# Eight-core recurrence and ternary layer: transposing DMAs issued by ScalarE, and the fourth pair's statistics taken earlier

## The reference

```
xn  = (x - mean(x)) / sqrt(var(x) + 1e-5)            # per row
a   = tanh(xn @ Wa.T + ba);  b = tanh(xn @ Wb.T + bb)  # [4096, 64]
h_t = a_t * h_(t-1) + b_t                            # a scan over the 4096 rows
y1  = xn + h @ Wout.T + bout
s   = mean(|weight|)                                 # weight [2048, 2048]
w_t = clip(round(weight / (s + 1e-10)), -1, 1) * s
y   = x + y1 + xn @ w_t.T + bias
```

## Time and profile before

| What | us |
|---|---|
| Runs: median (lowest to highest of 3) | 548.99 (546.73 to 550.02) |
| The profiled execution's own time | 545.46 |
| Its span, slowest core (core 3) | 543.9 |
| Spans of the other cores | 535.8 (core 0) to 543.6 (core 7) |
| TensorE busy, core 3 | 467.0 (86% of the span) |
| VectorE, ScalarE, GpSimd busy | 341.8, 215.8, 150.3 |
| SyncE's DMA queue, share of 16 engines' span | 61.3% |
| TensorE waiting in front of gate products, core 3 | 12.4 in 5 waits |

### The profile page before, as it was taken

One profiled execution on the slowest core, in us unless ns is written; L12 is line 12 of the kernel. 1 busy time (PEld: TensorE's weight loads), 2 busy tenths in 40 slices (PEclk: granted clock), 3 DMA queues, 4 the chain that ended last, 5 costly groups with the idle time before them and its releaser, 6 DMA issues.

```text
span 543.9 us, 8281 instructions; the slowest of 8 cores (535.8 to 543.9 us)
## 1 busy us (share of the span) xinstructions
PE 467.0 (86%) x2323; PEld 223.9 (41%) x2323; DVE 341.8 (63%) x516; ACT 215.8 (40%) x183; POOL 150.3 (28%) x536
## 2 busy tenths in 40 slices
PE   0020489999939999999999999999999999999997
PEld 0010134545424444444444545454545444545443
DVE  2633497969737574857576767666666757573633
ACT  0477395745434334252506070706161615242000
POOL 0400236331634051414233232323241415150000
PEclk9999999999979999999999999999999999999999
DMA  7999980264464948585777667676858584843212
GB/s 225 341 331 344 303 217 1 78 218 112 117 144 152 209 156 219 149 221 156 221 158 213 174 183 205 189 199 174 215 164 224 160 228 155 232 145 88 107 49 116
DMA packets 72048, 99.15 MB, mean 182 GB/s; under 512 B 57090, under 2 KB 57090, under 8 KB 65986
## 3 DMA queue, kind: packets, MB, share of 16 engines
q1 hardware_dynamic: 71328, 97.53, 61.3%
q0 software_dynamic: 384, 1.05, 1.2%
q10 hardware_dynamic: 292, 0.05, 0.1%
HBM read 52.48 MB, written 33.55 MB: 158 GB/s over the span
## 4 chain that ended last, share of the span: by engine, by line
PE 57%; DMA 15%; SPq 10%; issue 4%; POOLq 4%; DVE 4%; ACT 3%; DVEq 2%; POOL 0%; ACTq 0%
PE pu L714 44%; DMA wbuf<-wt 6%; DMA xnT<-wbuf 5%; PE pu L686 5%; PE pab L673 4%; SPq L265 4%; SPq L257 3%; DMA y<-sx 3%; DVE bst L439 2%; ACT wbuf L337 2%; DMA sx<-x 1%; SPq L270 1%; DVEq L441 1%; PE pu L732 1%; PE pu L727 1%
## 5 line engine op out<-in xcount | busy, mean ns | idle before, releaser
L455 DVE SCALAR_TENSOR_TENSOR sx<-pu,scl,sx 128x512 f32<-128x512 f32 x212 | 158.0, 748 | 147.1 <-PE pu L714 80.0
L714 PE MATMUL pu<-wbuf 128*128 128x512 f16 x896 | 204.7, 379 | 0.0
L714 PE MATMUL pu<-wbuf,xnT 128*128 128x512 f16 x672 | 154.2, 379 | 0.0
L714 PEld LDWEIGHTS pu<-wbuf 128*128 128x128 f16 x896 | 87.5, 98 | 103.3
L714 PEld LDWEIGHTS pu<-wbuf,xnT 128*128 128x128 f16 x672 | 65.6, 98 | 79.6
L439 DVE BATCH_NORM_STATS2 bst<-sx 128x6 f32<-128x512 f32 x128 | 78.8, 678 | 14.4 <-DMA sx<-x 14.2
L337 ACT ACTIVATE wbuf<-sx,nmr,yr 128x2048 f16<-128x2048 f32 x26 | 54.3, 2088 | 37.6 <-DMA xnT<-wbuf 31.2
L840 POOL TENSOR_SCALAR uu<-mv 128x1 f32<-128x1 f32 (+1 forms) x29 | 10.1, 348 | 209.5 <-DVE mv L443 201.1
L344 ACT ACTIVATE sx<-sx,nmr,p1r 128x2048 f32<-128x2048 f32 x32 | 66.9, 2093 | 2.4
L686 PE MATMUL pu<-wbuf,xnT 128*128 128x512 f16 x256 | 57.9, 379 | 3.7 <-DVE wbuf L490 2.0
L356 ACT ACTIVATE sa<-pab,bab_s 64x256 f32<-64x256 f32 x16 | 7.5, 468 | 117.8 <-PE pab L673 117.8
(11 more groups left out here) (62 smaller groups left out, 309.6 us busy)
## 6 DMA issues: line engine op xcount, KB each, us to landing
sx<-x SPq DMA_DIRECT2D x32, 1024.0 KB, 6.5
y<-sx SPq DMA_DIRECT2D x63, 512.0 KB, 3.7
wbuf<-wt SPq DMA_DIRECT2D x15, 1024.0 KB, 30.3
wbuf<-wt SPq DMA_DIRECT2D x2, 512.0 KB, 33.5
xnT<-wbuf SPq DMA_TRANSPOSE x52, 3.5
wab_s<-wab POOLq DMA_DIRECT2D x1, 512.0 KB, 12.7
y<-sx SPq DMA_DIRECT2D x2, 256.0 KB, 2.5
wocv<-wo POOLq DMA_DIRECT2D x1, 256.0 KB, 14.6
```

The source lines that it names most:

```text
L455: vector.scalar_tensor_tensor(out, bank(b), scl[:, :], out, OP.mult, OP.add).then_inc(s_ev, 1)
L714: ins = tensor.matmul(bank(b), left(p, lname, c), right(rname, c, h), start=(fresh and c == 0), stop=(state is None and c == HC - 1), skip ...
```

## The change

SyncE no longer issues turns. The function `turn` is ScalarE's now, with the same two waits and the same two transposing DMAs, and ScalarE calls it behind norm and ahead of resid, for the even and for the odd tile. What is left on SyncE for pair p is load(2p+5), load(2p+4) and four stores. For the fourth pair three things are moved: on VectorE stats(7) goes ahead of the last two `t3` steps and stats(6) behind unit 10; on GpSimd the chains of tiles 7 and 6 go ahead of the wait for unit 14 and of the `wo2` DMAs; on ScalarE norm(7) goes from behind states(2) to just ahead of resid(5), and turn(7) follows states(2).

```diff
@@ SyncE
-            def turn(t):
-                sync.wait_ge(s_xnb, POS[t] + 1)
-                sync.wait_ge(s_unit, last_use(t - 4))
-                for half in range(2):
-                    sync.dma_start_transpose(
-                        out=xT(t, half * HD, (half + 1) * HD).rearrange(
-                            "p (c w) -> p c w", c=HC),
-                        in_=xnb[:, half, :]).then_inc(s_dt, 16)
...
-            turn(7)
             for p in range(2, NP):
-                n, m = p + 1, p + 2
+                m = p + 2
                 a, b = 2 * p, 2 * p + 1
                 if m < NP:
                     load(2 * m + 1)
-                if n < NP:
-                    turn(2 * n)
-                if m < NP:
                     load(2 * m)
                 store(a, 0, HD, unit_no(p, 3))
                 store(b, HD, D, unit_no(p, 9))
-                if m < NP:
-                    turn(2 * m + 1)
                 store(b, 0, HD, unit_no(p, 11))
@@ ScalarE
+            def turn(t):
+
+                scalar.wait_ge(s_xnb, POS[t] + 1)
+                scalar.wait_ge(s_unit, last_use(t - 4))
+                for half in range(2):
+                    scalar.dma_start_transpose(
+                        out=xT(t, half * HD, (half + 1) * HD).rearrange(
+                            "p (c w) -> p c w", c=HC),
+                        in_=xnb[:, half, :]).then_inc(s_dt, 16)
...
                     evict_T(b, 1)
+                    if n == 2:
+                        norm(7)
                     resid(b)
                 else:
                     norm(a)
+                    turn(a)
                     resid(a)
                 gates(n)
                 states(n)
-                if TURNED // 2 <= n + 1 < NP:
+
+                if 4 <= n + 1 < NP:
                     norm(b + 2)
+                if 3 <= n + 1 < NP:
+                    turn(b + 2)
                     resid(b + 2)
@@ VectorE
             plain(9)
+            stats(ORD[6])
             t3(4)
             t3(6)
             plain(10)
+            stats(ORD[7])
             plain(11)
-            stats(ORD[6])
-            stats(ORD[7])
@@ GpSimd
             chain(4, 5)
+            for t in ORD[TURNED:TURNED + 2]:
+                chain(t, t)
 
             g.wait_ge(s_unit, 14)
             g.wait_ge(s_T, 8)
             g.dma_start(out=wo2[0:64, :], in_=wo_d[:, HD:D]).then_inc(s_wo2, 16)
             g.dma_start(out=wo2[64:128, :], in_=wo_d[:, HD:D]).then_inc(s_wo2, 16)
-            for t in ORD[TURNED:]:
+            for t in ORD[TURNED + 2:]:
                 chain(t, t)
```

## The result

The changed kernel takes 665.27 us (median of 4 runs, 661.64 to 691.06), the kernel before, run beside it, 548.03. The forecast was 543.0 with a range of 537 to 560. The time lies outside it, on the slower side, and also beyond the 554 to 568 us of rival B.

What follows compares the result with a forecast made beforehand. TensorE's waits before gate products were taken as the bound; core 3 gains 3.7 at the fourth gate and 3.7 later, core 7 3.7 and 2.0, so the slowest core is 6.0 us shorter: 548.99 to 543.0 us, range 537 to 560.

Steps and rivals of the forecast that it cites:

- rival B: Even turns land only after both loads of the other queue: 2.2 us at 11 gates, 554 to 568 us; chance 0.21.
- What bounds the kernel: TensorE sets the end and waits only before gate products for transposing DMAs: 12.4 us on core 3, 11.2 on core 7.
- the change can win at most what these waits hold: Limit on the gain: TensorE's waits before gate products, 12.4 us on core 3; nothing else of the change touches TensorE.
- Statistics and chains: Fourth pair: stats and chains of tiles 7 and 6 moved up at cost 0, chains ending at 131 to 133 and 139 to 143.
- near 174: 0, and the cover is 27 us: GpSimd's `wo2` DMAs, put behind the chains, are wanted only near 174, so the move costs 0 with 27 us of cover.
- The 6.9 us from issue to use: Even turn on ScalarE beside two loads reaches its gate in 6.9 us; fourth gate -3.7 us, tile 10 ready 1.4 us early.
- half of a load of some 4 us put to the 4.9: How 6.9 us was reached: 4.9 us for an even turn alone plus half of a 4 us load beside it.
- a value over 8.3 with a wait before every gate: Sign of rival B: even turn needs over 8.3 us from issue, with a wait in front of every gate.
- Rivals A and C: A: turns beside loads take as long as behind, 546.5 us, chance 0.25; C: turns hardly notice loads, 539.6 us, 0.12.
- Issuing from ScalarE at 0: ScalarE issuing the 24 later transpositions costs 0, since the work behind is wanted later and ScalarE idled there.

Runs made afterwards that it cites:

- experiment 6: Against the changed kernel: loads from tile 8 cut into four DMAs of 2 KB rows, 691.32 us; or ScalarE's transposing DMAs replaced by plain copies, 604.21 us.
- Experiments 4 and 5: 4: first part alone, later loads issued by GpSimd, turns on SyncE, 649.81 us. 5: changed kernel, loads cut to 64 columns, 545.30 us; stores too, 542.14 us.

## Why the prediction was wrong

**What bounds the kernel: right.** TensorE waits only in front of gate products, before and after, and the loss is in those waits and in the clock behind them. What I did not draw from it: "the change can win at most what these waits hold" bounds the gain and not the loss.

**Statistics and chains: the times right, the cost of the moved DMA wrong.** The chains ended at 133.8 and 143.8 (forecast 131 to 133 and 139 to 143), norm(7) ran at 134.01 (133), gates(2) at 138.00 (137.2). What failed is the term for the `wo2` DMAs, "near 174: 0, and the cover is 27 us". The cover hid the transfer's own landing. It did not hide what the transfer does to others, since I put it where turn(7) is in flight: 4.8 us on a turn on the path. So turn(6) was issued at 154.50 and not at 149.5, and the fourth gate waited 10.2 us on core 2 and 13.7 over the cores, where 4 to 5 had been forecast (on cores 1, 4 and 6 turn(7) took 23 to 24 us). Moving a step means naming what it now runs beside.

**The 6.9 us from issue to use: the step that failed the prediction.** I took "half of a load of some 4 us put to the 4.9" for an even turn beside two loads of another queue; over the cores it was 13.9. The three even turns with rows above needed 9.0 us (154.50 to 163.47), 13.3 (187.34 to 200.62) and 23.6 (266.70 to 290.30). The forecast said a value over 8.3 with a wait before every gate would show rival B, and it did: 12 waits in the row above, none of them at the last gate, behind which no load was left. Rivals A and C needed turns of 8 us and less; they are out.

**Rival B: the right place and sign, too small.** It made 2.2 us for each of 11 gates. On core 2 the waits from gate 4 on sum to 96.7 us (106.9 less 10.2), 8.8 a gate. Its picture of small rows taking turns with large ones shows in the trace: from 232 to 234 the packet records of core 2 hold 49 rows of the turn's queue and 49 records of SyncE's, 46 of them of 4 or 8 KB. Two terms were missing. It added up bytes at the full rate of 257 to 307 GB/s, but in the stretches above a transposition and the other queue's loads and stores move together at 99 to 144; experiment 6 says that about half of the loss needs the transposition. And it priced no clock: that a gate behind a long wait runs at the lower one I had seen at the fourth gate, and counted only as something to win back. Here it cost 27 us.

**Issuing from ScalarE at 0: right.** With next to nothing beside the turns the kernel runs at 0.987, without a wait from gate 4 on, although ScalarE issues all 52 transposing DMAs.

**What the rules named would have given.** The Trainium skill (DMA: Bandwidth & Descriptors, "Issuing engines are not separate DMA queues") says issuing from several engines saves only the issue time. Experiments 4 and 5 agree that the issuer doesn't matter. But the rule knows only a gain or nothing, and here 21% were lost: the second queue took away an order that the single queue had kept. The Trainium skill (same page, "Rules for kernel authors") states that a transposition next to ordinary DMAs needs nothing; it stands in a row on transposing streams that corrupt each other's data. Of the data no run here says otherwise; for time, the runs do.

Open: what in the DMA engines makes a transposition and another queue's traffic slow each other. The records show few rows of either queue moving, at a share of 0.38 in one stretch and with many packets open at once in another, not which part stands still.

## What to carry to other kernels

Before a DMA is moved to another queue, list what its old queue kept it apart from; the order in a single queue may be a schedule that the kernel lives on. Keep transposing DMAs in one queue with the bulk transfers that are in flight with them, or hold those transfers back by a semaphore; a small transfer of another queue (256 KB here) can be enough to delay one. Where a wait on the path lengthens, price the matmuls behind it at the lower clock as well.

## What the hardware showed that I had not expected

A turn of 512 KB takes 4.5 to 4.8 us with next to nothing beside it, 6.1 beside another queue's stores, and 13.9 beside its loads (all over the cores); a single half took up to 22.5. It does so with turns from ScalarE and loads from SyncE, and with turns from SyncE and loads from GpSimd (14.8). While this lasts the core's DMA engines can move as little as 99 GB/s. The same loads cut into four DMAs of 2 KB rows made it worse: 1.257, against 1.211 with 8 KB. A plain copy in the same 256 B rows is delayed as well, but leaves the engines at 335 to 350 GB/s.
